# Six layer norms moved into the block of the projection behind each, and x loaded in four pieces

## The reference, cut to what matters

```python
def _layernorm(x, axis=-1, eps=1e-05):
    m = jnp.mean(x, axis=axis, keepdims=True)
    v = jnp.var(x, axis=axis, keepdims=True)
    return (x - m) / jnp.sqrt(v + eps)

# the six sublayers, in order, with the names of the kernel
# a: x = x + self_attention(ln(x))           16 heads, causal
# x: x = x + cross_attention(ln(x), ctx)     16 heads, 375 keys
# f: grouped attention of rms(ln(x)) with rotation, then a mixture of 32 experts
# b: x = x + self_attention(ln(x))           32 heads, rotation, bias
# y: x = x + gated cross_attention(rms(ln(x)), ctx)
# z: x = x + w_down(silu(w_gate h) * (w_up h)), h = ln(x)
```

## Time and profile before

| | |
|---|---|
| time, median of 3 runs | 2547.4 us (2547.07 to 2547.83) |
| the profiled execution's own time | 2552.67 us |
| its span, first to last instruction | 2551.1 us |
| mean granted TensorE clock | 0.949 |
| PE busy | 2311.6 us, 91% |
| DVE, ACT, POOL busy | 50%, 29%, 35% |
| DMA | 190.83 MB, mean 75 GB/s |

### The profile page before, as it was taken

How to read it: one execution, slowest core, us unless ns; L and a number is a source line. 1 busy time by engine, 2 the same in 40 slices (tenths; PEclk the granted TensorE clock), 3 DMA queues, 4 the chain that set the end, 5 groups by cost and what they waited for, 6 DMA issues and landing times. The chain is left out here.

```text
span 2551.1 us, 39942 instructions
## 1 busy us (share of the span) xinstructions
PE 2311.6 (91%) x15006; PEld 1685.6 (66%) x15006; DVE 1264.0 (50%) x2242; ACT 733.9 (29%) x1436; POOL 884.1 (35%) x689
## 2 busy tenths in 40 slices
PE   5888999587999999889999999968887999979998
PEld 5657877375878787644444444447666777758997
DVE  3564666645666767542222222266764466653333
ACT  1232232234444444221111111112542233222221
POOL 1332111145566666314444444324433111012220
PEclk9998999798999999989999999978998999979999
DMA  4002000021212110156666869640002100002110
GB/s 122 23 12 92 26 26 14 11 86 41 70 34 71 46 58 17 57 188 158 146 143 167 239 168 265 130 132 31 2 2 78 54 25 25 2 25 75 50 49 29
DMA packets 54754, 190.83 MB, mean 75 GB/s; under 512 B 7428, under 2 KB 7684, under 8 KB 47940
## 3 DMA queue, kind: packets, MB, share of 16 engines
q1 hardware_dynamic: 34400, 138.99, 16.1%
q0 software_dynamic: 19488, 47.05, 9.6%
q10 hardware_dynamic: 692, 2.42, 0.3%
HBM read 157.36 MB, written 31.06 MB: 74 GB/s over the span
## 5 line engine op out<-in xcount | busy, mean ns | idle before, releaser
L1960 PE MATMUL bank<-m_ring,m_bT 128*128 x696 | 317.9, 600 | 2.1 <-ACT m_bT L1707 0.9
L1960 PEld LDWEIGHTS bank<-m_ring,m_bT 128*128 128x128 f32 x696 | 126.0, 191 | 132.1 <-issue 131.0
L1899 DVE SCALAR_TENSOR_TENSOR m_prod<-bank,m_slot_rows,m_silu 128x256 f32<-128x256 f32 x87 | 42.1, 483 | 288.6 <-ACT m_silu L1694 288.6
L1658 POOL DMA_INDIRECT m_slot_rows<-m_rows,m_idx x87 | 86.2, 991 | 256.6 <-DVE m_prod L1899 209.0
L1666 POOL DMA_INDIRECT m_sum<-m_yb,m_idx x87 | 137.9, 1585 | 84.9 <-DVE m_yb L1907 84.4
L1694 ACT ACTIVATE m_silu<-bank 128x256 f32<-128x256 f32 (+1 forms) x95 | 36.4, 383 | 451.1 <-PE bank L1960 451.1
L1981 PE MATMUL bank<-m_ring,m_aT 128*128 x348 | 163.8, 593 | 1.0 <-DVE m_aT L1913 1.0
L237 PE MATMUL bank<-f_hT_hi,f_w_hi 128*128 128x448 f32 x288 | 122.4, 425 | 17.6 <-POOL f_w_lo L1223 13.5
L811 ACT ACTIVATE y_att_p_rows<-bank,y_att_n_top 112x375 f32<-112x375 f32 x128 | 71.6, 572 | 190.4 <-DVE y_att_n_top L853 190.4
L1230 POOL TENSOR_TENSOR f_att_turned<-f_att_turned,consts 128x448 f32<-128x448 f32 x64 | 77.5, 1212 | 127.0 <-ACT f_att_turned L1289 127.0
L237 PE MATMUL bank<-f_att_wo_hi,f_att_oT_hi 128*112 128x512 f32 x256 | 105.5, 412 | 11.8 <-issue 11.2
(11 more groups left out here) (481 smaller groups left out, 5773.4 us busy)
## 6 DMA issues: line engine op xcount, KB each, us to landing
m_ring<-in_m_w SPq DMA_DIRECT2D x32, 1536.0 KB
f_raw<-in_f_wq SPq DMA_DIRECT2D x64, 256.0 KB, 2.6
z_raw<-in_z_w SPq DMA_DIRECT2D x7, 1536.0 KB, 6.3
f_att_wo_raw<-in_f_wo SPq DMA_DIRECT2D x16, 512.0 KB, 5.8
x_c_raw<-in_ctxT SPq DMA_DIRECT2D x8, 752.0 KB, 4.2
y_c_raw<-in_ctxT SPq DMA_DIRECT2D x8, 752.0 KB, 4.2
m_sum<-m_slot_rows SPq DMA_DIRECT2D x2, 2048.0 KB, 16.4
a_raw<-in_a_wqk SPq DMA_DIRECT2D x8, 256.0 KB, 2.7
```

The source lines that it names most:

```text
L1658: pool.indirect_dma_start(rows[:, n % 3, :], None, rows_dram[:, :], bass.IndirectOffsetOnAxis(ap=idx[:, n:n + 1], axis=0)).then_inc(rows_i ...
L1960: o = pe.matmul(ps_gu[u % 2][0:m, :], lhs(k), weights(2 * EI * k), start=(k == 0), stop=(k == KC - 1))
```

## The change

`normalise` becomes a class `Norm` whose parts are called inside the blocks of `project` and `experts`, ahead of their own work on each engine. The block boundary between norm and projection goes; the clearing of the norm's semaphores moves behind the projection. The transposes use all eight banks and wait for no low part. ACT makes the high parts of the first two sequences before it splits the first weights. PE begins the projection when four low parts are done, with both weight tiles on the first half of the tokens: (u0,t0), (u1,t0), (u0,t1), (u1,t1) in the first pair. What waits for a unit of that pair waits by `done_by`. In stage a, x is loaded in four pieces of two sequences, each with its own semaphore; all early transfers are on SP's queue, the small ones behind the first weights; the small block is done in the projection's `meanwhile`. The instructions of the first pair are written out in front of each loop.

```diff
-def normalise(nc, g, name, src, kind, eps2=0.0, w=None, keep=None, early=None,
-              first=False, ahead=()):
...
+class Norm:
+    def sync(self, sp):
+        if self.first:
+            for dst, src, arrived in self.first.loads:
+                sp.dma_start(dst, src).then_inc(arrived, 16)
+        self.early.load(sp, self.early_in)
+        for dst, src, arrived in self.ahead:
+            sp.dma_start(dst, src).then_inc(arrived, 16)
+
+    def vector(self, dve):
...
+            if self.first:
+                if b % 2 == 0:
+                    dve.wait_ge(self.first.x_in[b // 2], 16)
+                dve.bn_stats(g.stats[:, b, :], src[:, b, :]).then_inc(self.stats_done, 1)
...
+    def scalar(self, act):
...
+        for b in range(2):
+            transposed_high(b)
+        self.early.split_high(act, self.early_in, self.early_hi)
+        for b in range(2, B):
+            transposed_high(b)
+
+    def tensor(self, pe):
...
+        for b in range(B):
+            pe.wait_ge(ready, b + 1)
+            for k in range(KC):
+                t = pe.transpose(g.bank[b][:, k * S:(k + 1) * S], self.y[:, b, k * P:(k + 1) * P],
+                                 g.const("ident")[0:S, 0:S])
+            t.then_inc(self.tr_done, 1)
...
         def each_pair(e, body):
 
-            with e.Fori(0, M // 2 - 1) as i:
-                body(i, False)
+            body(0, False)
+            if M > 4:
+                with e.Fori(1, M // 2 - 1) as i:
+                    body(i, False)
             body(M // 2 - 1, True)
+
+        def done_by(i, r):
+
+            return (1, 3, 3, 4)[r] if isinstance(i, int) and i == 0 else 4 * i + r + 1
...
+            norm.sync(sp)
             for u in range(2):
+                sp.wait_ge(norm.early_lo, u + 1)
                 sp.dma_start(raw[:, u, :], w_dram[2 + u]).then_inc(raw_in[u], 16)
...
                     if not last:
-                        act.wait_ge(mm_done, 4 * i + 2 * u + 2)
+                        act.wait_ge(mm_done, done_by(i, 2 * u + 1))
                         split_high(i + 1, u)
...
         @block.tensor
         def _(pe):
-            with pe.Fori(0, M // 2) as i:
...
+            norm.tensor(pe)
+            for t in range(NH):
+                pe.wait_ge(norm.lo_done, HB * (t + 1))
+                for u in range(2):
+                    pe.wait_ge(norm.early_lo, u + 1)
+                    unit(0, u, t)
+            with pe.Fori(1, M // 2) as i:
                 for u in range(2):
                     pe.wait_ge(lo_done, 2 * i + u + 1)
...
             def body(e, slot, first, last):
+                if first:
+                    pe.wait_ge(norm.early_lo, NP_)
+                    pe.wait_ge(norm.lo_done, HB)
                 pe.wait_ge(lo_done, NP_ * (e + 1))
                 gate_up(e, slot, 0)
...
-        with nc.Block() as block:
-            @block.sync
-            def _(sp):
-                sp.dma_start(x[:, :, :], a["x"].rearrange("b s d -> s b d")).then_inc(x_in, 16)
-                sp.dma_start(consts[:, :], a["consts"]).then_inc(x_in, 16)
-                sp.wait_ge(x_in, 32)
...
+        first = First(loads=[(x[:, 2 * i:2 * i + 2, :], a["x"][2 * i:2 * i + 2].rearrange("b s d -> s b d"), pair_in[i])
+                             for i in range(B // 2)] + [(consts[:, :], a["consts"], consts_in)],
+                      x_in=pair_in, consts_in=consts_in)
```

More of the change, by code:

```diff
@@ L156, in _ @@
[L156 to L188, removed]
-            for b in range(B):
[L190 to L205, removed]
@@ L223, in _ @@
-        @block.tensor
-        def _(pe):
-            for b in range(B):
-                pe.wait_ge(ready, b + 1)
-                if b >= 4:
-                    pe.wait_ge(lo_done, b - 3)
-                for k in range(KC):
-                    t = pe.transpose(g.bank[b % 4][:, k * S:(k + 1) * S], y[:, b, k * P:(k + 1) * P],
-                                     g.const("ident")[0:S, 0:S])
-                t.then_inc(tr_done, 1)
+        self.g, self.src, self.kind, self.eps2, self.w, self.early, self.ahead, self.first = (
+            g, src, kind, eps2, w, early, ahead, first)
@@ L235, in mm3 @@
+    def tensor(self, pe):
+        g, ready = self.g, self.h_done if self.kind == "ln" else self.y_done
+        if self.first:
+            pe.wait_ge(self.first.consts_in, 16)
+        for b in range(B):
+            pe.wait_ge(ready, b + 1)
[3 more added lines that the diff above has]
+            t.then_inc(self.tr_done, 1)
 def mm3(pe, out, w_hi, w_lo, x_hi, x_lo, first, last):
@@ L239, in mm3, with project @@
     return pe.matmul(out, w_lo, x_hi, start=False, stop=last)
-def project(nc, g, name, w_dram, M, out, weights, bias=None, scale=None, rope=None, value=None, also=None,
-            early=None, meanwhile=None):
+def project(nc, g, norm, name, w_dram, M, out, weights, bias=None, scale=None, rope=None, value=None, also=None,
+            early=None, meanwhile=None, needs=None):
     with ExitStack() as ctx:
@@ L398, in _, with body @@
         def _(dve):
+            norm.vector(dve)
             dve.sem_inc(out_done, 4)
-            with dve.Fori(0, M // 2) as i:
+            if needs:
+                dve.wait_ge(needs, 16)
+            def body(i, last):
                 for u in range(2):
@@ L446, in _, with unit @@
         def _(pe):
-            with pe.Fori(0, M // 2) as i:
+            def unit(i, u, t):
+                r = 2 * u + t
+                for k in range(KC):
+                    x = mm3(pe, g.bank[r][:, 0:HT], w_hi[:, u, k * P:(k + 1) * P], w_lo[:, u, k * P:(k + 1) * P],
+                            g.hT_hi[:, k, t * HT:(t + 1) * HT], g.hT_lo[:, k, t * HT:(t + 1) * HT],
+                            k == 0, k == KC - 1)
+                x.then_inc(mm_done, 1)
+            norm.tensor(pe)
[5 more added lines that the diff above has]
+            with pe.Fori(1, M // 2) as i:
                 for u in range(2):
@@ L2096, in _, with experts @@
                 shared_down(b)
-def experts(nc, g, name, w_dram, E, acc, weights, shares_dram=None):
+def experts(nc, g, norm, name, w_dram, E, acc, weights, shares_dram=None):
     U = NH * NC
@@ L2265, in body @@
                 gate_up(e, slot, 1)
+                if first:
+                    pe.wait_ge(norm.lo_done, B)
                 gate_up(e, slot, 2)
```

184 lines of the change are left out of this document (98 added, 86 removed).

## The result

| | before | after |
|---|---|---|
| median | 2547.24 us (2545.14 to 2547.83, 4 runs) | 2510.5 us (2507.04 to 2518.76, 4 runs) |
| the profiled execution, its span | 2552.67, 2551.1 us | 2511.44, 2509.6 us |
| mean granted clock | 0.949 | 0.959 |

The ratio is 0.9854, 95% interval [0.9837, 0.9872]: 1.5% faster. The forecast was 2524, its range 2511 to 2531. The change saved 36.7 us where 23.5 were forecast; rival A's 2510 is the time that came. "The changed kernel" is the kernel after, and the profile of it is this one where no other is named.

The account below looks back on a forecast made before the run. TensorE was busy nearly throughout, so its standing still around the norms counted. Savings of 31.2 us less 2.8, 3.5 and 1.4 gave 23.5, from 2547.4 to 2524; own range 2518 to 2529, with 2511 to 2531 also covering B and half of A.

Parts of the forecast that it names:

- rival A: In the norms, gapless transposes raise TensorE's clock and units start at full rate: 13.7 us more saved, about 2510; chance 0.10.
- the transposes at half rate: In the norms, transposes stay at half clock even without gaps: 0.81 us per token row group, 6.5 us for eight.
- the phase: When TensorE's clock rises in six stages: 1 us allowed for all, in the range only.
- Stages x and b: First unit follows the gapless transposes directly: 4.8 us saved in x, 5.0 in b.
- Stages f and y: With h multiplied by a weight row, the first unit waits for low part four: 3.75 us saved in each.
- Stage a: At the start, x in pieces lets h begin at 14.0 and the first unit at 21.15: 12.3 us saved.
- rival B: In stage a, x's pieces don't arrive in order, so 6.2 us are saved instead of 12.3: 2530; chance 0.09.
- Stage z: First expert's weights arrive late and TensorE waits for all three low parts: only 1.6 us saved.
- The moved clearing: Norm semaphores cleared behind a barrier after the projection: costs 0.46 us, six times, 2.8 in all.
- The first pair's order: Both weights on the first half of tokens first: TensorE waits before the fifth unit, costing 1.9 us in f, 1.6 in b.
- C: Rotated stages f and b stall at every pair, clock down each time: 9.8 us more, 2534; chance 0.04.
- D: Written-out first pairs need instruction fetches; waits without a releaser in six stages cost 44 us: 2568; chance 0.03.

Follow-up runs that it names:

- The first experiment: The kernel before, with only the norms' transposes changed to use eight banks and wait for no low part: 2544.56 us, ratio 0.9982.
- the second: The changed kernel, eight banks kept, with transposes of sequences four to seven again waiting for low parts: 2518.05 us, ratio 0.9888.
- the fastest version: The changed kernel with the old first-pair order, norm and projection semaphores cleared together, z's first gate unit waiting for two of three weight pieces: 2498.73 and 2497.04 us.

## Why the prediction was wrong, point by point

**The step that failed** is the clock: the transposes at half rate, "eight tokens' rows at 3.25/4 = 0.81 take 6.5 us", and above all the first matmuls behind them, which the sum left at half rate with "the phase", for which I allowed 1 us. Those matmuls brought 10.2 us where the sum has nothing; the forecast missed by 13.2, and its other errors nearly cancel. I had the mechanism as rival A and gave it 0.10. Against it I had set the Trainium skill, page "TensorE: Matmul & The Clock Gate", section "Part 4: PE-mode transpose", by which the full rate doesn't engage for transposes. Here the measurement differs and decides: 0.50, 0.63, 1.00 in consecutive stretches with nothing else on TensorE. And the trace of before could have told. I wrote that each norm's stretch shows "0.50 with 32 transposes". That holds for x, f, b and y, but not for z (TensorE's busy us, granted clock, DMA share, GB/s):

```profile
2286.20:2289.40 3.20, 3.18 (x16) 0.50 0.75 301
2289.50:2292.80 3.30, 0.00 (x0) 1.00 0.00 0
2292.90:2297.30 4.40, 3.18 (x16) 0.50 0.00 0
```

TensorE had been idle for 6.2 us before the first of these rows, so one burst of 16 transposes was followed by full clock, which then ran out in the gap of 4.7 us. Those rows spoke against the rule, and nothing but the rule held the chance down to a tenth.

What it brought: the first 14 matmuls of a to y, 25.0 us before and 14.8 after, 10.2 (A: 11.5). The first experiment shows that transposes without gaps bring nothing for these matmuls while a pause follows them (25.0 again), and the second that without the pause most of it comes even with the gaps (17.5). So the missing pause is the larger part, the missing gaps the smaller. z, which kept its pause, kept its slow start, and lost it when the pause was filled. Rival A's sum had only the gapless transposes as the cause; by its own rows, 5.1 less 14x0.205, it comes to 2.2 a stage and 11.2, not 11.5.

**Stages x and b**, 4.8 and 5.0: measured 6.0 and 6.1. The transposes end after 4.9, and then low part four decides, as A had it. Low parts took 0.55 each, not 0.65.

**Stages f and y**, 3.75 each: measured 5.9 and 6.5. I let h win 1.9 and the product lose 1.9. Only the first happened: eight products took 5.39, the last three of them beside POOL's subtractions, and it was POOL that was held, 4.02 for two that take 2.5 alone. The two stages came out 2.2 and 2.7 above the sum, a little more than the bound of 1.9; low parts of 0.55 instead of 0.65 make up to 0.4 of that. The choice between the bounds was wrong; my row was of an addition, and additions still are held (f's next pair: two in 6.25 beside POOL's 4.99). The means over eight hide what happens. Single instructions of f (ns, shortest/median/longest), h in the kernel before, then POOL's subtractions in the kernel after:

```profile
L177 DVE TENSOR_SCALAR f_x<-x,f_norm_mv,f_norm_rstd x8: 533/540/2946, 491.1 to 496.7; 112x512 f32<-112x512 f32 x8
...
L115 POOL TENSOR_TENSOR f_w_lo<-f_raw,f_w_hi x2: 1270/2027/2784, 475.8 to 478.6; 128x512 fp32r<-128x512 f32 x2
```

Before, one h stood until both subtractions were done and the other seven were undisturbed. After, POOL's first subtraction began at 475.85, in the run of products, and ended at 478.63, 1.1 us behind the last of them; the products took 0.75 each throughout.

**Stage a**, 12.3: measured 12.8. Order of the queue, x's landing, h at 14.0 (14.13) and the transposes (6.18 for 6.5) were right; rival B is out. The Trainium skill, page "DMA: Bandwidth & Descriptors", section "Queues, rings and completion order", has each DMA engine take a ring's descriptors in order. The pieces of x, which came in order and 1.65 us apart, agree with that. **Stage z**, 1.6: 2.2.

**Costs.** The moved clearing at 0.46: 0.5, right. The first pair's order: waits of 1.9 and 1.6 forecast, 2.2 and 2.05 measured, in the place named and released by the addition named. What the clock lost behind each was 1.6 (7.5 less 4.25, halved), not 0.7: I took half of a row, and the full row, 1.4, was nearer. C was out: no further pair stalls, and a, x and y have no wait. D was out: waits without a releaser are three, as before.

**Not in the sum at all**: z's experts 4.1 us longer (0.7 of it the first 14 matmuls behind the pause, the rest the open distance), and the end of z 2.3 longer, of which 0.8 is the barrier and the rest a last burst of matmuls that ran slower in both profiles of after, down to 0.50, and didn't in one of the fastest version's (20.8 us as before). I take that for the moment at which the clock falls; no run tests it.

**The sum as measured**: h to unit and the start 39.5 (forecast 31.2), the first matmuls 10.2 (0), first pair's order -7.5 (-4.9), barriers -3.0 (-2.8), z -4.1 (0) and its end -1.5 (0): 33.6. The two profiles of each kernel lie 35.6 apart; the rest I put down to the attention and expert parts, which vary by some microseconds between executions (f's: 1153 to 1158 us in the same kernel).

That rival A's 2510 is so near is in part luck. Its cause is the one that was missing, but f and y gained 4.9 more than it had, and the first pair's order and z cost 8.2 that it hadn't.

## What to carry to other kernels

Count a pause of TensorE twice: for its length, and for the half-rate matmuls behind it, which here cost 10.2 us beside the 13.4 of waiting. Before you let a rule set a chance, read the granted clock of every stage for a row that speaks against it: one stage of six had it here. And look whether closing one pause only moves the next one (eight banks alone gave 0.2%). When an order is turned to start one unit earlier, follow the first buffer that is needed again: here the turned order gained nothing and cost 7 us. Where VectorE and POOL hold each other up, take the price from a row of the same operation, and look at single instructions: the mean over eight hides that one of them stood for the whole of the other engine's work.

## What the runs showed of the hardware that I had not expected

- Transposes alone bring the granted clock from 0.50 to 1.00: in the kernel before behind one burst of 16 (stage z), in the gapless bursts of 32 the rise came 3.1 to 6.5 us after the first. A pause of 5.2 us behind them lost it and one of 2.6 didn't, while behind f's wait of 2.2 it fell: the length alone doesn't decide.
- When a POOL subtraction (two tiles in SBUF) meets VectorE, one of the two stands until the other is done. h (two scalars per token, one SBUF input) stood: 2.95 instead of 0.54 for the one that met two subtractions, 3.74 to 5.65 for eight. The addition of two SBUF inputs stood: 5.05 for the one that began beside POOL's 4.99, where 0.75 or 0.9 is usual. A run of products (a scalar and two SBUF inputs) did not: 0.75 each, and POOL's subtraction took 2.78 instead of 1.26.
- At full clock the same matmuls stand 202.7 or 206.7 ns apart, for dozens to a thousand at a time. The value differs between executions of one kernel (stage x of the kernel before: 202.7 and 206.7) and can change inside a stage.
